# Softmax shares all on ScalarE, the conditioning's last product on GpSimd, in a fused conditioning, attention and expert kernel

## The reference

```
decay = exp(-exp(w)) * (0.5 + 0.5*tf)           # tf = sigmoid(sum(cond)), one per sequence
ek = exp(min(f, 30));  a_t = a_(t-1)*decay + ek_t*f_t;  b_t = b_(t-1)*decay + ek_t   # forward and backward
num = nf + nb - ek*f + exp(min(u+f,30))*f
den = df + db - ek   + exp(min(u+f,30))
cond(x) = sigmoid(x) * num / max(den, 1e-8) * (0.8 + 0.2*tf)
x = x + attention(cond_0(x))                    # 16 heads of 128, causal softmax, output projection
x = x + experts(cond_1(x))                      # 8 experts of 256 x 256, gates from the top 2 logits
```

## Time and profile before

| | |
|---|---|
| median of 3 runs | 371.82 us (371.78 to 371.84) |
| the profiled execution's own time | 371.82 us |
| its span in the profile | 369.9 us, so 1.9 us lie around it |
| mean granted TensorE clock | 0.995 of full speed |
| instructions | 7426 |

### The profile page before, as it was taken

The page is one execution under the profiler, slowest core; times in us unless marked ns, Lnnn a source line. Parts: engine busy times, 40 slices in busy tenths (PEclk is TensorE's granted clock), DMA queues, the critical chain, the costliest instruction groups (busy, mean ns, idle before and its releaser), DMA issues.

```text
span 369.9 us, 7426 instructions
## 1 busy us (share of the span) xinstructions
PE 344.7 (93%) x2404; PEld 319.4 (86%) x2404; DVE 318.7 (86%) x892; ACT 255.9 (69%) x687; POOL 212.6 (57%) x223
## 2 busy tenths in 40 slices
PE   0796599999999999999999999999999989899997
PEld 0685499998999999989999999999999979788885
DVE  4979899999898989899989999999768576869675
ACT  5669888788878869886888888878778565321100
POOL 1875686855756468867867886787673424210000
PEclk9999989999999999999999999999999999999999
DMA  5670130100000000130100022100000000000000
GB/s 166 240 276 4 57 113 2 59 4 1 2 0 3 1 2 0 52 123 0 28 31 3 1 73 101 58 3 1 2 2 1 2 1 2 0 16 15 28 28 30
DMA packets 4613, 14.13 MB, mean 38 GB/s; under 512 B 848, under 2 KB 1888, under 8 KB 3936
## 3 DMA queue, kind: packets, MB, share of 16 engines
q1 hardware_dynamic: 4352, 13.66, 11.0%
q10 hardware_dynamic: 224, 0.01, 0.0%
HBM read 12.60 MB, written 1.05 MB: 37 GB/s over the span
## 4 chain that ended last, share of the span: by engine, by line
PE 63%; DVE 28%; ACT 3%; issue 3%; DMA 1%; DVEq 0%; ACTq 0%
PE psQK L947 7%; PE psQK L949 7%; PE psQK L948 7%; DVE tiles L729 4%; PE psT L1017 4%; PE psO L947 3%; PE psS L947 3%; PE psS L949 3%; PE psS L948 3%; PE psO L949 3%; PE psO L948 3%; PE psV L947 3%; PE psS L1003 3%; PE psZ L1030 3%; PE psV L948 3%
## 5 line engine op out<-in xcount | busy, mean ns | idle before, releaser
L324 POOL TENSOR_SCALAR prob<-prob,rsum 128x256 f32<-128x256 f32 x60 | 55.5, 925 | 63.1 <-DVE rsum L764 63.1
L947 PE MATMUL psQK<-y_hi,w_hi 128*128 128x256 f32 x256 | 72.2, 282 | 1.1 <-DVE y_lo L679 1.1
L518 ACT ACTIVATE prob<-prob,ntop 128x256 f32<-128x256 f32 (+1 forms) x128 | 57.0, 448 | 23.1 <-DVE ntop L756 23.0
L949 PE MATMUL psQK<-y_hi,w_lo 128*128 128x256 f32 x256 | 72.3, 282 | 0.0
L948 PE MATMUL psQK<-y_lo,w_hi 128*128 128x256 f32 x256 | 72.2, 282 | 0.0
L330 POOL TENSOR_TENSOR z_lo<-z_lo,z_two 128x256 fp32r<-128x256 f32 x64 | 48.2, 753 | 33.7 <-DVE z_lo L782 33.7
L289 POOL TENSOR_TENSOR w_lo<-raw,w_hi 128x512 fp32r<-128x512 f32 x40 | 53.7, 1352 | 11.2 <-ACT w_hi L383 11.1
L947 PEld LDWEIGHTS psQK<-y_hi,w_hi 128*128 128x128 f32 x256 | 48.6, 190 | 2.9 <-issue 1.5
L948 PEld LDWEIGHTS psQK<-y_lo,w_hi 128*128 128x128 f32 x256 | 48.6, 190 | 1.3
L949 PEld LDWEIGHTS psQK<-y_hi,w_lo 128*128 128x128 f32 x256 | 48.7, 190 | 0.0
L506 ACT ACTIVATE qk<-psQK 128x512 fp32r<-128x512 f32 x64 | 37.6, 587 | 15.1 <-PE psQK L949 14.8
(11 more groups left out here) (166 smaller groups left out, 1039.1 us busy)
## 6 DMA issues: line engine op xcount, KB each, us to landing
raw<-in_weights SPq DMA_DIRECT2D x5, 1024.0 KB, 5.3
raw<-in_weights SPq DMA_DIRECT2D x10, 512.0 KB, 4.2
out<-fT SPq DMA_DIRECT2D x8, 128.0 KB, 1.7
fT<-in_fT SPq DMA_DIRECT2D x2, 256.0 KB, 5.0
xT<-in_xT SPq DMA_DIRECT2D x2, 256.0 KB, 6.8
fT<-in_fT SPq DMA_DIRECT2D x1, 512.0 KB, 6.2
xT<-in_xT SPq DMA_DIRECT2D x1, 512.0 KB, 6.2
temb<-in_temb ACTq DMA_DIRECT2D x1, 1.0 KB, 3.3
```

What stands on the lines that cost most here:

```text
L324: pool.tensor_scalar(prob[:, k, P:3 * P], prob[:, k, P:3 * P], rsum[:, k, 1:2], None, ALU.mult).then_inc(shared, 1)
L518: ins = act.activation(prob[:, k, lo:hi], prob[:, k, lo:hi], ACT.Exp, scale=-1.0, bias=ntop[:, k, q:q + 1], accum_out=ssum[:, k, q:q + 1])
L947: pe.matmul(out, ah, bh, start=first and k == 0, stop=False)
L949: ins = pe.matmul(out, al, bh, start=False, stop=last and k == n - 1)
```

## The change

SHARES_ACT is gone: in every unit ScalarE scales both pieces of the shares, first the 128x256 one and then the 128x128 one, and GpSimd none. One semaphore, `shared`, tells TensorE. The product `y` goes from DVE to POOL, at the same offsets, as a plain tensor_tensor without the scale. The scale is put into the denominator: `rout` and `rhalf`, the reciprocals of the scales of layer 0 and 1, are made once on DVE before the first qk_low, and are used as scale and bias of the second instruction of `e1` (layer 0) and as second operand of the clamp of `den` (layer 1).

```diff
-COND_DVE, COND_ACT, COND_POOL = (13, 13), (9, 7), (5, 5)
+COND_DVE, COND_ACT, COND_POOL = (12, 12), (9, 7), (6, 6)
-POOL_PLACES = {"ekv": -1, "clamp": 2, "den": 3, "eukv": 4, "num": 5, "y_low": 8}
+POOL_PLACES = {"ekv": -1, "clamp": 2, "den": 3, "eukv": 4, "num": 5, "y": 7, "y_low": 8}
-SHARES_ACT = (0, 1, 2, 3)
@@ gpsimd
+            def y():
+                pool.wait_ge(c_dve[k], d0 + 12)
+                pool.wait_ge(c_pool[k], p0 + 5)
+                pool.tensor_tensor(t[:, XN] if w == 0 else cols(num2, b), t[:, XN], t[:, GD], ALU.mult).then_inc(c_pool[k], 1)
-        def shares(u):
-            k = u % 2
-            pool.wait_ge(recipd, u + 1)
-            pool.tensor_scalar(prob[:, k, P:3 * P], prob[:, k, P:3 * P], rsum[:, k, 1:2], None, ALU.mult).then_inc(shared, 1)
-            if u not in SHARES_ACT:
-                shares(u)
@@ scalar
-                act.activation(t[:, EK], t[:, EK], ACT.Copy, bias=1.0).then_inc(c_act[k], 1)
+                act.wait_ge(scales_done, 1)
+                act.activation(t[:, EK], t[:, EK], ACT.Identity, scale=rout[:, b:b + 1], bias=rout[:, b:b + 1]).then_inc(c_act[k], 1)
-                act.wait_ge(c_dve[k], d0 + 13)
+                act.wait_ge(c_pool[k], p0 + 6)
-            act.activation(prob[:, k, 0:P], prob[:, k, 0:P], ACT.Copy, scale=rsum[:, k, 0:1]).then_inc(first_shared, 1)
-            if u in SHARES_ACT:
-                act.activation(prob[:, k, P:3 * P], prob[:, k, P:3 * P], ACT.Copy, scale=rsum[:, k, 1:2]).then_inc(shared, 1)
+            act.activation(prob[:, k, P:3 * P], prob[:, k, P:3 * P], ACT.Copy, scale=rsum[:, k, 1:2])
+            act.activation(prob[:, k, 0:P], prob[:, k, 0:P], ACT.Copy, scale=rsum[:, k, 0:1]).then_inc(shared, 1)
@@ vector
-                    dve.tensor_scalar(t[:, XD], t[:, XD], 1e-8, None, ALU.max).then_inc(c_dve[k], 1)
+                    dve.wait_ge(scales_done, 2)
+                    dve.tensor_scalar(t[:, XD], t[:, XD], 1e-8, rhalf[:, b:b + 1], ALU.max, ALU.mult).then_inc(c_dve[k], 1)
-            def y():        # scalar_tensor_tensor with tout (w == 0) or thalf (w == 1), at DVE_PLACES (7, "M")
...
+        dve.reciprocal(rout[:], tout[:]).then_inc(scales_done, 1)
+        dve.reciprocal(rhalf[:], thalf[:]).then_inc(scales_done, 1)
```

More of the change, by code:

```diff
@@ L52 @@
 COND_START = (None, None, 5, 13, 21, 29, 37, 45)
-COND_DVE, COND_ACT, COND_POOL = (13, 13), (9, 7), (5, 5)
+COND_DVE, COND_ACT, COND_POOL = (12, 12), (9, 7), (6, 6)
 DVE_PLACES = {"min": (-3, "E"), "xd": (0, "M"), "xn": (1, "M"), "gd": (2, "M"), "gn": (3, "M"), "den": (4, "M"),
-              "r0": (5, "M"), "r1": (6, "M"), "y": (7, "M")}
+              "r0": (5, "M"), "r1": (6, "M")}
 ACT_PLACES = {"exps": (-2, "E"), "sxd": (0, "E"), "sxn": (1, "E"), "e1": (2, "E"), "yhi": (7, "E")}
-POOL_PLACES = {"ekv": -1, "clamp": 2, "den": 3, "eukv": 4, "num": 5, "y_low": 8}
-DVE_FIRST = {"xd": (0, "M"), "xn": (0, "E"), "gd": (1, "M"), "gn": (1, "E"), "den": (2, "M"), "r0": (2, "E"), "r1": (3, "M"), "y": (4, "M")}
+POOL_PLACES = {"ekv": -1, "clamp": 2, "den": 3, "eukv": 4, "num": 5, "y": 7, "y_low": 8}
+DVE_FIRST = {"xd": (0, "M"), "xn": (0, "E"), "gd": (1, "M"), "gn": (1, "E"), "den": (2, "M"), "r0": (2, "E"), "r1": (3, "M")}
 ACT_FIRST = {"sxd": (0, "E"), "sxn": (1, "M"), "e1": (1, "E"), "yhi": (4, "E")}
-POOL_FIRST = {"ekv": 0, "clamp": 1, "den": 2, "eukv": 3, "num": 4, "y_low": 5}
+POOL_FIRST = {"ekv": 0, "clamp": 1, "den": 2, "eukv": 3, "num": 4, "y": 4, "y_low": 5}
 REFILL = {1: (("qk", 0, -1), ("qk", 1, 0), ("v", 0, 1), ("qk", 2, 2), ("v", 1, 2), ("qk", 3, 3), ("o", 0, 5), ("o", 1, 8)),
@@ L103, in build @@
     thalf = sb("thalf", [P, B], F32)
+    rout = sb("rout", [P, B], F32)
+    rhalf = sb("rhalf", [P, B], F32)
     ew = sb("ew", [P, 2, CB], F32)
@@ L184, in build @@
     expert_done, expert_half, expert_read, stored = (sem(n) for n in ("expert_done", "expert_half", "expert_read", "stored"))
-    last_half, first_shared = sem("last_half"), sem("first_shared")
+    last_half, scales_done = sem("last_half"), sem("scales_done")
     gT_ready, bias_high, bias_low, bias_moved = (sem(n) for n in ("gT_ready", "bias_high", "bias_low", "bias_moved"))
@@ L317, in num @@
                 pool.tensor_tensor(t[:, XN], t[:, GN], t[:, EKV], ALU.add).then_inc(c_pool[k], 1)
-            return {"ekv": ekv, "clamp": clamp, "den": den, "eukv": eukv, "num": num, "y_low": lambda: y_low(n)}
-        def shares(u):
-            k = u % 2
-            pool.wait_ge(recipd, u + 1)
-            pool.tensor_scalar(prob[:, k, P:3 * P], prob[:, k, P:3 * P], rsum[:, k, 1:2], None, ALU.mult).then_inc(shared, 1)
+            def y():
+                pool.wait_ge(c_dve[k], d0 + 12)
+                pool.wait_ge(c_pool[k], p0 + 5)
+                pool.tensor_tensor(t[:, XN] if w == 0 else cols(num2, b), t[:, XN], t[:, GD], ALU.mult).then_inc(c_pool[k], 1)
+            return {"ekv": ekv, "clamp": clamp, "den": den, "eukv": eukv, "num": num, "y": y, "y_low": lambda: y_low(n)}
         def z_last(u):
@@ L729, in recip @@
                 dve.reciprocal(t[:, GD, c], t[:, XD, c]).then_inc(c_dve[k], 1)
-            def y():
[L732 to L737, removed]
             return {"min": clamp, "xd": xd, "xn": xn, "gd": gd, "gn": gn, "den": den,
-                    "r0": lambda: recip(0), "r1": lambda: recip(1), "y": y}
+                    "r0": lambda: recip(0), "r1": lambda: recip(1)}
         def y2_last(b):
-            n = 4 + b
-            dve.wait_ge(c_dve[n % 2], cond_base(n, COND_DVE) + COND_DVE[1])
+            n = 6 + b % 2
+            dve.wait_ge(c_pool[n % 2], cond_base(n, COND_POOL) + COND_POOL[1])
             dve.wait_ge(tanh_done, b + 1)
@@ L888, in _ @@
         first_y_low(1)
+        dve.wait_ge(pre_act, 5)
+        dve.reciprocal(rout[:], tout[:]).then_inc(scales_done, 1)
+        dve.reciprocal(rhalf[:], thalf[:]).then_inc(scales_done, 1)
         dve.wait_ge(consts, 2 + E)
@@ L1007, in turn @@
         def turn(u):
-            pe.wait_ge(first_shared, u + 1)
             pe.wait_ge(shared, u + 1)
```

## The result

The changed kernel takes 374.26 us (median of 7 runs, 374.07 to 374.95), the kernel before, in runs on the same chip, 371.82 us. The ratio is 1.0069 with a 95% interval of 1.006 to 1.0078: slower by about 2.5 us. The forecast was 373.0 us. The execution that was profiled took 374.78 us, 0.5 us above the median; its span is 372.9, against 369.9 before.

The account below looks back on a forecast made before the run. TensorE was taken as the bound, busy 344.7 of 369.9 us, with only its waits to win or lose. Terms 0.4 + 0 + 0.35 + 0.25 + 0.1 + 0.1 = 1.2 us gave 373.0 us; range 371.0 to 374.5.

Parts of the forecast that it names:

- B: Rival: DVE, relieved of y, reaches v_low earlier and psV's three waits go; about 369.8 us, chance 0.13.
- C: Rival: ACT does not recover between units in four stretches, z_last also late in 27, 35, 43; 376.2 us, chance 0.12.
- The forecast's mechanism: ACT's extra 0.41 us per share delays the next unit's pT_high and, where DVE already waits for it, passes to DVE.
- Shares cost 0.41 us of ACT each, and POOL's relief starts nothing: All 60 moved shares: ACT gains 25 us of work; POOL loses 55.5 us, which by itself starts nothing earlier.
- Unit 7, +0.35: Units 6 and 7: pT_high, z_low and the output projection run back to back, so +0.35 us (0 to 0.4).
- Unit 22, +0.25: Shares of 19 and 20 delay pT_high 0.8 us; 0.4 to 0.5 reach v_low of unit 21: +0.25 us.
- Unit 14, +0.1: Queue at unit 13, mostly hidden by POOL's y_low, which blocks the scans anyway: +0.1 us (0 to 0.4).
- Unit 28, +0.4 as a wait in unit 30: Later pT_high and qk_high in unit 28 cost DVE 0.54 us; TensorE's wait in unit 30 grows +0.4 (0 to 0.8).
- Units 36 and 44, 0: DVE's relief from y is eaten whole by ACT's later qk_high: 0 us (-0.4 to +0.1).
- Operands, +0.1: Scale and bias from SBUF in e1's second instruction, unit 1: 0.14 us for two, +0.1 in the sum (0 to 0.2).
- The signs of being wrong: Next profile: psV's waits gone or halved, TensorE waits in units 27, 35, 43, or stretched scans short all over the middle.
- Rival A: ACT's idle time absorbs the 0.41 us everywhere, DVE's relief covers unit 28: 371.8 us, at most 0.5 either way; chance 0.2.

## Why the prediction was right or wrong

The direction was right, and 374.26 lies in the stated range (371.0 to 374.5), near its upper end. It lies outside the forecast's own range (372.2 to 374.0), and just above the sum with every term at its high end (374.2). The size was half of what was measured (1.2 against 2.4 us), so that the range held is in part owed to the width that B and C had given it.

The forecast's mechanism, ScalarE's later pT_high, is shown by the kernels that have it alone and that lack it. Of the sum, 1.1 us were for the shares, where the shares alone measured 1.3 to 1.6 us (median and ratio). What it lacked is the other half. y on GpSimd stood in it only as a relief of VectorE that might be eaten up; moved alone, with the shares where they were, it costs 1.0 to 1.2 us, of which 0.2 are the operands'. Point by point:

- **Shares cost 0.41 us of ACT each, and POOL's relief starts nothing.** The busy times came out as forecast within 5 us for ACT (278 against 283), exactly for POOL, and within 2 or 3 us for DVE (5.7 less, not 8). Taken by itself the relief is worth something in one stretch of the middle, 0.5 us in unit 30, as I had half seen (the scans met z_last), and in units 4 to 7, which I had not looked at for it. ScalarE's 128x128 piece now also stands behind the 128x256 one; no run tests this order by itself.
- **Unit 7, +0.35.** Measured +0.41: right, by pT_low and z_low as told: the output projection starts 3.28 us into the unit instead of 2.87. That two kernels with the same shares ahead of it show no such loss (above) was not foreseen.
- **Unit 22, +0.25.** Measured +0.62: mis-sized. I halved ScalarE's 0.8 us by judgement and took half the room from it. 0.67 us arrived at v_low, since VectorE was waiting for pT_high again, and the scans were stretched a little too (1.39 us against 1.27 for the two of before).
- **Unit 14, +0.1.** Measured +0.69: the step that failed worst. I said that POOL's y_low blocks the scans anyway and left it at that. What was missing is that y pushes everything behind it in GpSimd's queue, so that its next product lies on another instruction of VectorE's (0.28 us); that y_low itself comes later onto the scan (0.35 with y alone); and that ScalarE's delay is 0.26 us here as well.
- **Unit 28, +0.4 as a wait in unit 30.** Measured +0.29 for units 28 to 35: near in size by luck, wrong in place. It is +0.73 in unit 28 and -0.53 in unit 30. The prediction followed the later pT_high to qk_low and v_low alone. But pT_low comes 0.74 us later too, `turn` of unit 28 may not start before it, and the wait of unit 30 shrinks in return, 0.20 us where 1.1 was forecast.
- **Units 36 and 44, 0.** Measured +0.27 and +0.24 by stretch. The relief of y did count behind (unit 38 -0.21), it was not eaten whole; but `turn` of units 36 and 44 and the output projection of 39 and 47 lost more.
- **Operands, +0.1.** Measured 0.18 us per instruction where I took 0.14 from rows of other widths, and 0.2 us in units 2 and 3: the mechanism is right, at the high end of the term. The estimate of 0.19 us for both from the figure of the Trainium skill (ScalarE: Activation LUTs, What ACT_TABLE_LOAD costs) was nearer.
- **The signs of being wrong.** One of them came true without its rival: psV's recorded waits did go or halve (unit 30 from 0.73 to 0.20 us, none left in 38 and 46), and I had written "B" beside that. The kernel is slower all the same. In unit 30 TensorE arrives later, and what units 38 and 46 gave back (0.21 and 0.12 us) units 36, 39, 44 and 47 took. A shorter wait is a gain only if the unit and those ahead of it are no longer. DVE's waits for qk_high, forecast as longer, stayed (5.4 and 5.5 us).
- **Rival B** is refuted as a forecast for this change, though its cause is there: with the shares taken from both engines, y on GpSimd gives 370.05 us. **Rival A** needed ScalarE's pT_high to have time to spare everywhere; DVE's waits for it grew from 7.1 to 16.9 us. **Rival C** did not happen: no wait in units 27, 35 and 43, which are longer by 0.03 to 0.06 us.

## What to carry to other kernels

Work moved to an idle engine is paid at the places where a neighbour waits for that engine next; set the two traces side by side unit by unit, since the sums of the waits can stay the same while their places change. One unit alone is no price either: the next one may give the difference back. An instruction put into GpSimd's queue shifts all behind it, and each of these must be held against the two-input instructions of VectorE that it now lies beside. Relief and load that stand in one change are best moved place by place: the share of three units and the product of three conditionings gave 1.2 us, all of them together cost 2.5.

## What the runs showed of the hardware

- An 8x256 tensor_tensor on VectorE took 1.48 us beside a 128x512 product on GpSimd, and 0.35 us a unit earlier: here a small instruction was held back for about as long as the product ran (1.30 us).
- Scale and bias from SBUF made a 128x512 activation 0.18 us longer (0.816 against 0.633), and units 2 and 3 longer by the same (12.61 to 12.63 against 12.42).
- The place of the stretch at half clock shifts with small changes ahead of it: it began at 45.73 us before and at 40.87 with 12 more shares on ScalarE. Unit 5 took 5.80 us in the first and 4.31 in the second, unit 6 4.33 and 5.89; units 4 to 6 together took 15.54 and 15.52, so the shift was worth nothing.
